# First attention of a two-layer kernel: five roots on GpSimd, the reciprocal in halves, output products at other steps

## The reference

```
x = x + L0_xattn(layernorm(x), ctx)   # 16 heads, 256 positions, softmax, Wm and bm on top
x = x + L0_ffn(layernorm(x))          # softmax over 64 experts, best 8
x = x + L1_xattn(layernorm(x), ctx)
x = x + L1_ffn(layernorm(x))          # softmax over 16 experts, best 4

def _layernorm(x, axis=-1, eps=1e-05):
    m = jnp.mean(x, axis=axis, keepdims=True)
    v = jnp.var(x, axis=axis, keepdims=True)
    return (x - m) / jnp.sqrt(v + eps)
```

## Time and profile before

| | |
|---|---|
| median of 3 runs | 681.9 us (681.1 to 682.09) |
| the profiled execution | 680.48 us |
| its span, first to last instruction | 678.0 us |
| mean granted TensorE clock | 0.839 |
| busy in the span: PE, DVE, POOL, ACT | 481.2, 362.2, 368.8, 260.7 us |

### The profile page before, as it was taken

The page is one execution under the profiler, slowest core; times in us unless marked ns, Lnnn a source line. Parts: engine busy times, 40 slices in busy tenths (PEclk is TensorE's granted clock), DMA queues, the critical chain, the costliest instruction groups (busy, mean ns, idle before and its releaser), DMA issues.

```text
span 678.0 us, 12350 instructions
## 1 busy us (share of the span) xinstructions
PE 481.2 (71%) x3519; PEld 368.3 (54%) x3520; DVE 362.2 (53%) x1105; ACT 260.7 (38%) x621; POOL 368.8 (54%) x517
## 2 busy tenths in 40 slices
PE   2641898788888430699989996176674599999960
PEld 1530344344443210588878874165453599999950
DVE  6981675799985560145444443565744144444426
ACT  0351065566668210333323331133342355555520
POOL 9494311116666673156555556226666787777730
PEclk9785597899989655699999999566886699999985
DMA  5089989856579696789999733959922333333327
GB/s 187 0 204 232 338 308 281 236 105 186 169 248 281 205 406 280 218 250 329 327 311 323 264 118 111 390 217 338 401 74 88 94 106 103 106 97 95 128 63 288
DMA packets 78131, 144.15 MB, mean 213 GB/s; under 512 B 12639, under 2 KB 56687, under 8 KB 76289
## 3 DMA queue, kind: packets, MB, share of 16 engines
q1 hardware_dynamic: 52048, 86.41, 39.5%
q0 software_dynamic: 13968, 32.29, 13.0%
q10 hardware_dynamic: 12064, 24.84, 12.5%
HBM read 85.14 MB, written 66.78 MB: 224 GB/s over the span
## 4 chain that ended last, share of the span: by engine, by line
PE 33%; DMA 12%; DVE 5%; POOL 5%; issue 2%; ACT 1%; SPq 1%; POOLq 0%; DVEq 0%
PE sc_ps L1814 11%; DMA hd_side<-held 6%; PE hd_ps_up L1252 6%; PE sc_ps L1796 5%; DMA rows<-hd_side_out,hd_side_target 3%; PE hd_ps_out L1258 2%; DMA sc_rows<-rows 2%; PE hd_ps_x L1230 2%; PE sc_ps L1804 1%; POOL sc_n_root L1494 1%; PE sc_ps L1749 1%; PE sc_ps L1761 1%; POOL sc_n_full L1492 1%; POOL listed L688 1%; PE sc_ps L618 1%
## 5 line engine op out<-in xcount | busy, mean ns | idle before, releaser
L1027 DVE TENSOR_REDUCE at_top<-at_ps_top 128x2 f32<-128x512 f32 x128 | 83.0, 685 | 42.9 <-PE at_ps_top L932 41.8
L1399 POOL DMA_INDIRECT rows<-hd_out,hd_rows x64 | 62.2, 972 | 57.4 <-DVE hd_out L1350 37.6
L1099 ACT ACTIVATE at_prob<-at_ps_score 128x512 f32<-128x512 f32 x128 | 72.3, 594 | 47.8 <-PE at_ps_score L950 47.4
L1252 PE MATMUL hd_ps_up<-hd_x_turned,e_arena 128*128 128x160 f32 x512 | 82.9, 306 | 0.0
L1814 PEld LDWEIGHTS sc_ps<-sc_t_turned,sc_up_w 128*112 128x112 f32 x672 | 81.2, 181 | 2.6
L1814 PE MATMUL sc_ps<-sc_t_turned,sc_up_w 128*112 128x128 f32 x672 | 82.4, 277 | 0.0
L932 PE MATMUL at_ps_top<-e_arena 96*128 96x256 bf16 x256 | 55.4, 304 | 37.0 <-PEq L107 21.9
L1252 PEld LDWEIGHTS hd_ps_up<-hd_x_turned,e_arena 128*128 128x128 f32 x512 | 76.4, 193 | 8.7 <-issue 6.2
L688 POOL DMA_INDIRECT held<-e_extended,e_address x64 | 62.3, 973 | 25.4 <-issue 17.7
L1387 DVE TENSOR_TENSOR hd_inner<-hd_silu,hd_ps_up 128x160 f32<-128x160 f32 x64 | 20.6, 322 | 83.4 <-ACT hd_silu L1337 83.4
L1709 POOL DMA_INDIRECT listed<-sc_empty,sc_index x48 | 46.7, 974 | 14.6 <-issue 12.8
(11 more groups left out here) (267 smaller groups left out, 941.1 us busy)
## 6 DMA issues: line engine op xcount, KB each, us to landing
e_arena<-in_weights SPq DMA_DIRECT2D x52, 384.0 KB, 11.3
held<-e_empty ACTq DMA_DIRECT2D x16, 960.0 KB, 6.3
hd_rows<-held SPq DMA_DIRECT2D x15, 768.0 KB, 9.9
e_w<-in_weights SPq DMA_DIRECT2D x16, 704.0 KB, 10.1
sc_rows<-rows SPq DMA_DIRECT2D x8, 1024.0 KB, 7.3
sc_tile_rows<-listed SPq DMA_DIRECT2D x42, 144.0 KB, 2.2
parts<-op_parts SPq DMA_DIRECT2D x8, 576.0 KB, 6.4
e_arena<-in_weights ACTq DMA_DIRECT2D x12, 384.0 KB, 4.2
```

Source lines behind the costliest of these rows:

```text
L1027: nc.vector.reduce_max(top[:, 2 * h:2 * h + 2], ps_top[at % TOPS][:], AX_X).then_inc(top_found, 1)
L1099: nc.scalar.activation(prob[at % RING][:], ps_score[at % SCORES][:], ACT.Exp, scale=scale).then_inc(prob_ready, 1)
L1252: op = nc.tensor.matmul(ps_up[e % 2][:, part, :], w[:, k, part * P:(part + 1) * P], x_turned[g % 2][:, j, k, :], start=k == 0, stop=k == 1)
L1399: nc.gpsimd.indirect_dma_start(rows_out, to, out_ap, None, bounds_check=TOKENS * LAYER0.chosen - 1, oob_is_err=False).then_inc(semaphore, 16)
```

## The change

It has three parts.

1. For batches 0 to 4 the root moves from DVE to POOL, at the same step. On POOL it is three instructions: add the epsilon, raise to the power -0.5, multiply the mean. The Newton steps of `pool_scale` go. Batches 5 to 7 keep the root on DVE. POOL sets the exponent once ahead of the loop.
2. The reciprocal of 256 columns becomes two of 128, the first one step earlier. The wait for the packed load goes with the first half, so one step earlier too; the product waits for both halves.
3. The four half-groups of a pair move from rests 5, 7, 1, 3 (by eight steps, the last two in the next eight) to 7, 1, 2, 3. The first product of a pair is now three steps behind the step at which ACT keeps the pair before it, instead of one.

The diff:

```diff
@@ Rstd.pool_scale
-        nc, (full, square, work) = self.nc, (self.work[:, k:k + 1] for k in range(3))
+        nc, full = self.nc, self.work[:, 0:1]
         root, shift = self.scale[:, b % 2, 0:1], self.scale[:, b % 2, 1:2]
         pool.wait_ge(self.known, b + 1)
         link(nc.gpsimd.tensor_scalar(full, self.mean_var[:, 1:2], EPS, None, ALU.add))
         link(nc.gpsimd.tensor_tensor(root, full, self.power[:], ALU.pow))
-        for _ in range(NEWTON - 1):
-            link(nc.gpsimd.tensor_tensor(square, root, root, ALU.mult))
-            link(nc.gpsimd.tensor_scalar(work, square, full, -0.5, ALU.mult, ALU.mult))
-            link(nc.gpsimd.tensor_scalar(root, work, 1.5, root, ALU.add, ALU.mult))
         nc.gpsimd.tensor_scalar(shift, self.mean_var[:, 0:1], root, -1.0, ALU.mult, ALU.mult).then_inc(self.ready, 1)
@@ attend_phase, gpsimd
             operands.set_rows(nc, pool, DEEP - 1)
+            rstd.pool_start(link)
             for at in range(-LEAD, END + LEAD):
...
                     cut_tops(hh)
+                b = steps("scale", at)
+                if b is not None and b < B - 3:
+                    rstd.pool_scale(pool, link, b)
                 for b, k in steps.scatters.get(at, ()):
                     routing.pool_scatter(pool, b, k)
@@ attend_phase, tensor
-                if 4 <= at < B * H + 4 and at % 4 == 1:
-                    weigh(at // 4 - 1, 0)
-                if 4 <= at < B * H + 4 and at % 4 == 3:
-                    weigh(at // 4 - 1, 1)
+                for offset, late_group, half in ((7, 0, 0), (9, 0, 1), (10, 1, 0), (11, 1, 1)):
+                    p, late = divmod(at - offset, HALF)
+                    if late == 0 and 0 <= p < HALVES:
+                        weigh(2 * p + late_group, half)
@@ attend_phase, vector
+            def invert(b, half):
+                if half == 0:
+                    dve.wait_ge(packed_loaded[b % 2], 32 * (b // 2 + 1))
+                link.free(nc.vector.reciprocal(share[:, half * P:(half + 1) * P], packed[b % 2][:, 1, half * P:(half + 1) * P]))
+
             def divide(b):
-                dve.wait_ge(packed_loaded[b % 2], 32 * (b // 2 + 1))
-                link(nc.vector.reciprocal(share[:], packed[b % 2][:, 1, :]))
+                dve.wait_ge(link.semaphore, link.count)
...
+                b = steps("share", at + 1)
+                if b is not None:
+                    invert(b, 0)
                 b = steps("share", at)
                 if b is not None:
+                    invert(b, 1)
                     divide(b)
...
                 b = steps("scale", at)
-                if b is not None:
+                if b is not None and b >= B - 3:
                     rstd.dve_scale(dve, link, b)
```

## The result

| | before | changed |
|---|---|---|
| median | 681.5 us (680.12 to 682.09, 4 runs) | 670.95 us (669.01 to 673.11, 4 runs) |
| the profiled execution, its span | 680.48, 678.0 us | 669.01, 666.5 us |
| busy: PE, DVE, POOL, ACT | 481.2, 362.2, 368.8, 260.7 us | 479.4, 356.3, 375.0, 260.2 us |

The ratio is 0.9847, with an interval of 0.981 to 0.9885.

A forecast was written before the change was run, and what follows sets the result against it. DVE was taken as the limit, 17.76 us a batch. Gains of 0.4, 1.76, 0.96, 1.77, 0.52 (batches 0 to 4) and 0.35 (step 125) make 5.8; 680.48 less 5.8 is 674.7, plus 1.42 to the median 676.1, range 672.8 to 679.2.

The forecast's parts named there:

- if it comes again: Batch 3: its lower-clock stretch, costing 1.4, recurs, so PE needs 17.4 instead of 19.17; gain 1.77 us.
- DVE sets the period, then POOL does: Batches 1 to 4: DVE limits at 17.76; root moved, batch 1 takes 16.0, POOL holds batches 2 and 4 at 16.8.
- The long end of 2.9: Upper price in us of one root on POOL, with add and multiply at 1.10 each; 1.25 was taken.
- The terms of batches 1, 2 and 4: Gains between transposes 16 steps apart: 1.76 (17.76 to 16.0), 0.96 (17.76 to 16.8) and 0.52 us (17.32 to 16.8).
- lost at step 40 ... that transfer does not start earlier: Early output products: gains at steps 23 and 36 vanish as PE waits 0.79 for DMA rows until 129.73; priced 0.
- The three-head limit: Scores lead exponentials by at most three heads, so step 23's score stalls behind ACT's same copy instead of the product.
- the second copy, at step 36: ACT's next copy of a pair: whatever the moved products gain there is lost at step 40; priced 0.
- The tail: After the batches: all gates move with the scatters, which start about 5.8 us earlier at the same spacing.
- Nothing later changes: Behind the load of the expert rows: the sum holds no term, so 0 gain there.
- POOL doesn't hold the period: Rival, chance 0.15: batches 1 to 4 all run at 16.0, batch 3 sheds its slow clock; gain 8.7, 673.2 us.
- the products take the early stall away: Rival, chance 0.06: the 2.80 stall goes whole and step 40's rows come earlier; gain 8.6, 673.3 us.
- The slower rival: Rival, chance 0.06: POOL's root blocks batches 2 to 4, one us per us; kernel slower from a root of about 3.2.

The follow-up runs named there:

- newton: Changed kernel with two more refining steps of three small POOL instructions each after the root's power: 682.22 us, ratio 0.9998 to the kernel before.
- scatter_last: Changed kernel with the last scatter of batches 0 to 2 moved behind the next cutting of tops (step 76 instead of 73): 669.3 us, ratio 0.9833.
- scatter_first: Changed kernel with the last four scatters of batches 0 to 2 three steps earlier, ahead of the root on POOL: 675.55 us, ratio 0.9903.
- products_early: Kernel before with the new places of the output products for the first five pairs only (up to step 43): 679.78 us, ratio 0.9954.
- products_only: Kernel before with only the output products moved, three heads off from their pair's keeping: 677.83 us, ratio 0.9951.
- early2: Changed kernel with ACT issuing expert weight loads every two steps instead of three, 21 instead of 12 during the batches: 672.24 us, ratio 0.9856.
- pad: Changed kernel with 50 unused small DVE memsets at the end of DVE's part of the first attention: 673.31 us, ratio 0.9861.
- before_pool_pad: Kernel before with 15 unused small POOL memsets, three per batch in batches 0 to 4 at the root's step: 683.7 us, ratio 1.0024.

## Why the prediction was right or wrong

The span by stretches, in means of two profiles of the kernel before and three of the changed one, with the forecast's terms:

| stretch (starts of rows) | before | changed | gain | forecast |
|---|---|---|---|---|
| to the first score of step 0 | 86.0 | 85.3 | 0.7 | 0 |
| to the transpose of step 39 | 43.9 | 42.9 | 1.0 | 0 |
| to the transpose of step 111 | 80.6 | 73.1 | 7.5 | 5.4 |
| to the first of the 32 scatters | 13.6 | 13.3 | 0.2 | 0.35 |
| to the load of the expert rows | 48.7 | 48.0 | 0.7 | 0 |
| to the end | 407.2 | 405.1 | 2.1 | 0 |

These profiles differ by 12.3 us and the medians by 10.5, because the second profile of before, at 684.75, lies above the 681.5 from which the 10.5 is counted; so the gains of the rows are upper readings. The 0.7 ahead of step 0 is scatter: over all profiles that start lies between 84.1 and 86.7. The forecast fell short in three rows: the batches (7.5 for 5.4), the early stretch (1.0 for 0) and the end (2.1 for 0). Three steps failed with that: batch 3's term by its size, the products priced at nothing up to step 40, and nothing at all for what comes later; the first two have a cause on record, the last has none.

- *DVE sets the period, then POOL does.* Right in its numbers: 16.0 and 16.8 were forecast, 15.95 and 16.58 came; the root was priced 1.25 and took 1.26; newton's and scatter_last's periods show POOL's hold from both sides. That DVE alone is behind the 15.95 is not shown, since PE is by then as full as DVE. The long end of 2.9 did not show: beside DVE's maxima out of PSUM the three instructions kept 0.24, 0.57 and 0.27. That agrees with the rule of the Trainium skill (SBUF — State Buffer, section "SBUF: two separate sides") in the prediction. But scatter_first has the case in which that rule would let one wait for the other, a DVE instruction with two SBUF inputs beside the root's power, and both kept their lengths there (0.57 and 0.34; in the next two batches the power took 0.61 and 0.58):

```profile
166.22 0.57 POOL L555 TENSOR_TENSOR at_n_scale<-at_n_work,at_n_power 128x1 f32<-128x1 f32 x1
166.23 0.34 DVE L656 TENSOR_TENSOR_SCAN e_extended<-ones,more,e_mask 128x64 int32<-128x64 bf16 x1
```

So the short price is measured; that it is short because the maxima come from PSUM is not shown.

- *Batch 3, "if it comes again": the failed step, by its size.* I carried the lower clock of batch 3 over (17.4 after the change, a gain of 1.77). It did not come again: from transpose to transpose the batch took 19.17 and then 16.56, a gain of 2.61. The clock is the third number from the end (first before, then the changed kernel):

```profile
172.14:191.31 19.17, 16.38 (x146) 8.25 (x143) 16.47 (x43) 11.82 (x26) 11.06 (x22) 0.91 0.64 209
```

```profile
168.22:184.78 16.56, 14.94 (x142) 7.84 (x142) 14.70 (x33) 11.48 (x25) 12.29 (x25) 1.00 0.67 208
```

The terms of batches 1, 2 and 4 were nearer: 1.81, 1.17 and 0.75 in these two profiles, for 1.76, 0.96 and 0.52; batch 0, from step 39 to 47, gave 0.1 for 0.4. I also took the kernel before with one such stretch, as in its first profile; the second has three. Of the seven windows of ten microseconds from 130 to 200, the six kernels with the root on DVE show the clock below 0.95 in 14 of 42; the thirteen with the root on POOL in three instructions in 2 of 91. Each such period is 1.2 to 1.5 longer (18.96 and 19.23 against 17.76 in the second profile of before). So with the root on POOL nearly all of the slow stretches are gone too. That PE's waits bring them is shown for newton's long ones. For the root on DVE the traces fit it: each of the eleven falls of the clock between 133 and 200 begins 0.1 to 2.2 us behind the end of a PE wait of 1.16 to 1.25. But most such waits are followed by no fall (products_early has seven of them and none), so there it is only the likeliest reading.

- *The products, "lost at step 40 ... that transfer does not start earlier": failed.* The score of step 40 no longer waits (128.04), the stretch to step 39 is 1.0 to 1.5 shorter, and products_early, with the new places up to step 43 only, has as much gain as products_only. The three-head limit was right (2.30 at step 23). I took a wait of 0.79 for a wall, but the transfer behind it hangs on the transpose of step 31, which came at 116.57 before and 115.61 now, and it starts 0.9 earlier (SP's timeline, first before, then the changed kernel):

```profile
117.90 3.00 SPq L861 DMA_DIRECT2D e_arena<-at_top_rows  x3
```

```profile
116.99 2.52 SPq L857 DMA_DIRECT2D e_arena<-at_top_rows  x3
```

I also priced the second copy, at step 36, like the first, although PE had two more heads of work in hand there.

- *The tail.* Right in its gates (early2). The 0.7 in the table lies within the scatter of single profiles (47.6 to 49.0).
- *Nothing later changes: failed, and open.* Behind the load of the expert rows fourteen runs with the root on POOL, newton's among them, took 403.8 to 406.8 (mean 405.6), five with it on DVE 406.7 to 409.1 (407.6). These are groups found afterwards, not an experiment; pad speaks against one cause, before_pool_pad settles nothing.
- *The rivals.* "POOL doesn't hold the period" gave 673.2 and "the products take the early stall away" 673.3; the result lies beyond both, for neither's reason alone. The slower rival is real: newton meets it at a root of 3.3 us, with no gain left. That its point of 3.2 fits so well is luck: it was worked out from a gain of 5.8, not 10.5, and half of the price that newton paid is clock.

## What to carry to other kernels

When a step is moved to an engine with queued work, add up that engine's chain around it: it gave the new period to 0.2 us, and showed which queued transfer stood in the way. Do not carry a slow-clock stretch over into a kernel whose PE waits less, and do not take a wait seen at one place in one profile for a wall: ask of both whether the change moves what they hang on.

## What was not expected of the hardware

- A PE wait of 2.6 to 2.7 us was followed by a stretch at the lower clock level, and the next period was another 2.7 longer (18.68, then 21.36).
- The granted clock of the batches differed between executions of one kernel: below 0.95 in one of seven windows in the first profile of before and in three in the second. With the root on POOL in three instructions it was so in 2 of 91.
- A DVE instruction with two SBUF inputs ran for 0.34 us within a GpSimd power of 0.57 us, and neither took longer than elsewhere; in two more batches the power took up to 0.03 us more.
- Between the last scatter's end (257.30 in early2's timeline) and the load that waits for all of them (264.38) lie 7.1 us, the last four with no DMA traffic.
